# Scores from two float32r parts in quarters of the array's rows, and top-k values multiplied once a batch

## The chip, the cores and the metric

The kernel runs on one core of a Trainium2 chip. Its time is the device time of one execution in microseconds; before the change the median of three runs is 3110.93 us (3107.17 to 3118.0).

## The reference

The input is `hidden_states`, 8 batches of 1024 tokens by 128 channels, float32. Four blocks follow one another, each added to its input and each on a layer norm of it:

```
x = x + attn_a(layernorm(x))     # 16 heads of 8 channels, 1024 x 1024 softmax per head
x = x + ffn(layernorm(x))        # 128 -> 512 -> 512 -> 128, weights +1 or -1, relu
x = x + attn_b(layernorm(x))     # top-k attention, 8 heads of 16
x = x + ffn(layernorm(x))
```

In `attn_a`, q and k come from linear layers, the scores are `q k^T / sqrt(8)`, the softmax runs over all 1024 keys, and the result goes through `Wo`. In `attn_b` each token looks, for each head, at the 64 tokens up to itself. A weighted distance of queries is taken to each, the 32 nearest stay, with weights `exp(-distance)` divided by their sum, and the context is the weighted sum of the values `relu(x @ encoder_value)` of those tokens. It is multiplied by q and decoded.

## The kernel before

**Stages and turns.** Every stage of the work has a name and is written once for each engine (`go` in each engine's block), and one list of stages gives the order in which all engines issue. The lists are made by `merged` from slots with weights (`WEIGHTS`, line 119, `SPANS`, `TAIL_SPANS`); no engine departs from its list. The waits between engines are on semaphores (`Count`). A turn has two lists, one after the other. The first has the row maxima of attention for batch c (stage `max`, sides "a"), beside the last stages of attention for batch c-1 ("o"), the first FFN and the preparation of `attn_b` for c-1 ("p"), and the last FFN of c-2 ("q"). The second has the exponentials and the products with V (stages `exp`, `pvs`) of batch c, beside the top-k attention of c-1 (`SLOTS_T`: `aop`, `dist`, `dev`, `top`, `vw`, `wt`, `pv`, `st`, `dec` for each of 8 tiles of 128 tokens) and the layer norm, q, k and their splitting ("h") of batch c+1. Turns 0, 1 and 7 leave out what doesn't exist yet or any more, and a last list (`TAIL`) finishes batches 6 and 7.

**Scores.** q and k (float32) are each split into three bf16 parts (`qk` and `split`, 0 to 4): the leading part is rounded by ScalarE (ACT, line 1095), subtracted by GpSimd (POOL, 730, 733), the rest rounded again (1102) and subtracted again (737). The second half of the keys gets its sign turned as it is evicted, and the difference of the two halves, k(j) - k(j + 512), is made beside them (`kd`, 512 columns) and split in the same way. The parts are written to DRAM (`scratch_q`, `scratch_k`, lines 620 and 621) and read back into `Q` and `K`, eight rows for each part of a head, so that six products of parts are summed by one matmul: 48 rows a head (`QPART`, `KPART`, `MROW`; `load_quad`, 524). A quad is four heads; `Q[:, n, i]` holds two of them, one from row 0 and one from row 64 of the array, `par` 0 and 1, and i is 0 or 1. Rows 48 to 50 of each hold three parts of the negated maximum against rows of ones in K.

**Maxima.** A group g is 128 queries of two heads, 64 groups a batch, ordered by quad, then i, then query tile (`MAXES`, 153). PE computes for both heads the products with the key differences (512 columns, into PSUM pair 0) and the products with the far half of the keys (pair 1 or 2). ACT takes the relu of the first into `cut(g)` (line 1110), one of three slots; DVE subtracts the far products and takes the row maximum with one instruction per head (`cut_max`, 1243), for g-1 at the place of g in the list. Differences of g wait for the relu of g-1 (in turn 0, of g-2), far products of g for the maximum of g-2. Once a quad, `mrow` negates the maxima and splits them in three (five DVE instructions, 1323 to 1327), and `mturn` transposes them (876), and brings them through DRAM to the rows in Q.

**Exponentials.** A step (n, i) takes 128 keys of the quad's four heads against 512 queries: two `exp` stages, each two score matmuls of 51 rows (a PSUM pair) and one ACT exponential of 128x1024 (1123), and four products with V in column tiles of 32 (`pvs`), of which the profile shows eight records: a float32 matmul leaves two.

**Values of attn_b.** `xrev` is the layer norm's output, channels by tokens in reverse order, and its last column repeated 64 times. For each tile, `vw` multiplies four windows of 96 tokens of it with `ev` (the value encoder), and ACT evicts them with a relu into `Vw[:, n % 2]` (line 1183 calls `evict`, 1034). Neighbouring windows overlap by 64 tokens. `pv` multiplies the transposed weights `WT` with them; a column of ones beside each head's values gives the sum of the weights. `WT` lies in `Bs`, which stage `keys` uses before.

Of the kernel before, what the change touches and what calls it, by code (L numbers as in the profile page):

```python
# [22 lines left out]
P = 128  # L23
NB, T = 8, 1024
NU = T // P
HALF = 512
# [3 lines left out]
PARTS = 3  # L30
QPART = (0, 0, 0, 1, 1, 2)
KPART = (0, 1, 2, 0, 1, 0)
QLOAD = ((0, 3, 0), (3, 2, 1), (5, 1, 2))
KLOAD = ((0, 3, 0), (3, 2, 0), (5, 1, 0))
MROW = len(QPART) * HD
KT = T + HALF
# [26 lines left out]
            key=1, pad=1, an=1, qtok=1, hebb=1, dist=2, vw=1, wt=2, pv=1, st=1, dec=1)  # L63
# [46 lines left out]
def between(slots, *others):  # L110
# [5 lines left out]
    return slots  # L116


WEIGHTS = dict(O=(1.00, 0.33, 1.92, 1.58, 0.47, 1.50, 0.85, 0.85, 1.47, 2.53), P=(0.90, 0.90, 0.90, 0.90, 0.90, 0.90, 0.90, 1.08, 1.21, 1.08, 1.08, 0.63, 0.90, 0.90, 0.90, 0.39, 0.90, 0.90, 0.90, 0.90, 0.90, 0.90, 0.90, 0.90, 0.90, 1.00, 1.00, 1.00, 1.50, 0.90, 0.54, 1.08, 1.08, 1.08, 1.08, 1.08, 0.90, 0.44, 0.90, 0.90, 1.19, 1.19, 1.19, 1.19, 1.19, 1.19, 0.90, 0.90, 0.90, 1.00, 1.00, 1.00, 1.50, 0.90, 0.90, 0.90, 0.90, 0.90, 1.00, 2.00, 2.00, 1.00, 1.00, 1.00, 1.94, 2.00, 2.00, 0.48, 2.00, 2.21, 0.55, 1.10, 1.10, 1.11, 1.11), Q=(0.90, 0.90, 0.90, 0.90, 0.90, 0.90, 0.90, 1.08, 1.08, 0.75, 0.49, 1.08, 0.90, 0.90, 0.90, 0.90, 0.90, 0.90, 0.90, 0.90, 0.90, 0.90, 0.82, 0.90, 0.59, 1.00, 1.00, 1.05, 1.83, 0.05, 0.95, 1.01, 0.95, 0.90, 0.90, 0.90, 0.90, 0.90, 0.90, 0.90, 0.90, 0.90, 0.95, 0.90, 0.90, 0.90, 0.90, 0.90, 0.80, 0.90, 1.00, 1.00, 1.00, 2.18, 0.10), T=(2.57, 2.00, 2.66, 2.50, 2.00, 3.99, 1.50, 1.08, 2.57, 2.00, 2.66, 2.50, 2.00, 3.99, 1.50, 1.08, 2.57, 2.00, 2.66, 2.50, 2.00, 3.99, 1.50, 1.08, 2.17, 2.00, 2.66, 2.50, 2.00, 3.99, 1.50, 1.08, 2.57, 2.00, 2.66, 2.50, 2.00, 3.99, 1.50, 1.08, 2.57, 2.00, 2.66, 2.50, 2.00, 3.99, 1.50, 1.08, 2.57, 2.00, 2.66, 2.50, 2.00, 3.99, 2.28, 1.08, 2.57, 2.00, 2.66, 2.50, 2.00, 3.99, 1.50, 1.08, 2.57, 2.23, 2.66, 2.50, 2.00, 3.99, 1.50, 1.08, 0.86), H=(1.00, 0.75, 0.75, 0.44, 0.92, 2.48, 2.04, 1.00, 1.00, 1.00, 1.00, 0.50))
SPANS = dict(O=(0.010, 0.177), P=(0.382, 1.000), Q=(0.000, 0.453), T=(0.000, 1.000), H=(0.015, 0.300))  # L120


# [1398 lines left out]
```

## Time and profile before

| | before |
|---|---|
| runs, us | 3118.0, 3107.17, 3110.93 |
| profiled execution, us | 3113.11 |
| its span, us | 3111.4 |
| PE, DVE, ACT, POOL busy, us | 2513.3, 2152.0, 2328.1, 645.4 |
| mean granted TensorE clock | 0.907 |

Busy time is the union of an engine's instructions; the ends of matmuls are modelled, and two matmuls that run in different rows of the array overlap in it. The profile has weight loads as an engine of their own (PEld). The granted clock is a share of 2.4 GHz; 0.50 is 1.2 GHz. "Issue" among the idle times is time in which nothing that the profile shows was waited for.

### The profile page before, as it was taken

The numbers are of one execution on the slowest core, as the hardware profiler recorded it, in microseconds if no ns is written. First come the engines' busy times: TensorE is split into PE (matmuls) and PEld (weight loads), VectorE is DVE, ScalarE is ACT, GpSimd is POOL, SyncE is SP. The second block draws the span as 40 slices with busy tenths as digits, with TensorE's granted clock in tenths as the row PEclk, the third lists the DMA queues.
The fourth block names the chain that finished last, engine by engine and source line by source line (L and its number), as shares of the span: only waits on it lengthen the run. The fifth ranks groups of instructions, "written<-read, shape, count | busy, mean of one in ns | idle before, by whom it ended". The sixth has DMA issues, their size and how long they took to land.

```text
span 3111.4 us, 71098 instructions
## 1 busy us (share of the span) xinstructions
PE 2513.3 (81%) x21555; PEld 1153.9 (37%) x21555; DVE 2152.0 (69%) x10282; ACT 2328.1 (75%) x3241; POOL 645.4 (21%) x820
## 2 busy tenths in 40 slices
PE   4788788888788887888878887888878888887666
PEld 1112343344333443334433343334433344333454
DVE  5801778856786768956689467875679667982695
ACT  4798669967698677976689676995779877895433
POOL 3010114111241113301142012411124111311331
PEclk6599689999899998999999998998989999999888
DMA  2011001100011000100001000110001000000000
GB/s 87 25 45 39 2 9 40 34 18 6 9 47 34 12 13 11 51 28 9 9 33 38 18 9 9 40 34 19 12 2 60 27 8 2 9 2 1 1 8 8
DMA packets 60961, 67.50 MB, mean 22 GB/s; under 512 B 15602, under 2 KB 41908, under 8 KB 60580
## 3 DMA queue, kind: packets, MB, share of 16 engines
q1 hardware_dynamic: 60336, 62.29, 6.2%
q8 instruction: 195, 3.19, 0.4%
q14 instruction: 186, 1.52, 0.2%
q10 hardware_dynamic: 244, 0.49, 0.1%
HBM read 41.95 MB, written 20.71 MB: 20 GB/s over the span
## 4 chain that ended last, share of the span: by engine, by line
PE 38%; ACT 26%; issue 18%; DVE 11%; POOL 4%; SPq 2%; ACTq 0%; DVEq 0%; DMA 0%; POOLq 0%
PE banks L779 36%; ACT PT L1123 12%; DVE pq L1243 3%; POOL Aop L758 3%; ACT pq L1110 2%; PE banks L786 2%; ACT h L1135 2%; DVE xn L1460 1%; DVE h L1463 1%; ACT hparts L1134 1%; ACT Bs L1034 1%; ACT h L1034 1%; ACT xn L1066 1%; ACT h L1182 1%; DVE stat L1215 1%
## 5 line engine op out<-in xcount | busy, mean ns | idle before, releaser
L1123 ACT ACTIVATE PT<-banks 128x1024 f32<-128x1024 f32 x1024 | 999.9, 1035 | 85.2 <-PE banks L779 77.7
L1243 DVE CUSTOM_DVE_ANT_0 pq<-pq,banks 128x512 f32<-128x512 f32 x1024 | 656.7, 685 | 210.9 <-ACT pq L1110 164.5
L1110 ACT ACTIVATE pq<-banks 128x1024 f32<-128x1024 f32 x512 | 522.8, 1022 | 276.0 <-PE banks L779 252.6
L779 PE MATMUL banks<-PT,Vg 128*9 128x512 f32 x4096 | 550.4, 610 | 2.1 <-ACT PT L1123 2.1
L779 PE MATMUL banks<-Q,K 51*128 51x512 bf16 x2048 | 396.9, 394 | 175.8 <-ACT PT L1123 137.5
L779 PE MATMUL banks<-K,Q 48*128 48x512 bf16 x2048 | 376.3, 440 | 114.1 <-ACT pq L1110 63.9
L742 POOL TENSOR_TENSOR hparts<-h,hparts 128x512 fp32r<-128x512 f32 x112 | 140.2, 1272 | 1099.1 <-ACT h L1135 1099.0
L1460 DVE MATCH_REPLACE8 xn<-h,xn 128x96 f32<-128x96 f32 x1536 | 352.4, 243 | 0.0
L779 PE MATMUL banks<-hparts,W 128*128 128x512 f32 x1024 | 314.5, 437 | 37.1 <-ACT h L1135 30.8
L779 PEld LDWEIGHTS banks<-Q,K 51*128 51x128 bf16 x2048 | 109.5, 93 | 616.3 <-issue 584.6
L1463 DVE MAX8 h<-xn 128x8 f32<-128x96 f32 x1536 | 263.4, 244 | 0.3 <-issue 0.2
L765 POOL TENSOR_TENSOR h<-h,outside 128x768 f32<-128x768 f32 x64 | 116.7, 1823 | 643.9 <-DVE h L1443 643.9
L758 POOL TENSOR_SCALAR Aop<-qd,alpha,minus 128x128 f32<-128x128 f32 x512 | 227.1, 459 | 81.9 <-DVEq L1404 70.9
L779 PEld LDWEIGHTS banks<-hparts,W 128*128 128x128 f32 x1024 | 186.1, 200 | 138.8 <-issue 73.8
L779 PEld LDWEIGHTS banks<-K,Q 48*128 48x128 bf16 x2048 | 92.2, 96 | 371.1 <-issue 343.8
L1308 DVE TENSOR_TENSOR Vg<-banks,bvb 128x512 f32<-128x512 f32 x16 | 11.1, 692 | 180.6 <-PE banks L779 180.3
L779 PE MATMUL banks<-B,Aop 128*32 128x96 f32 x4096 | 109.6, 264 | 32.0 <-POOL Aop L758 29.4
L779 PE MATMUL banks<-xT,W 128*128 128x512 f32 x224 | 125.9, 674 | 8.7 <-ACT xT L1034 4.8
L1460 DVE MATCH_VALUE_LOAD xn<-h,xn 128x8 f32 x1536 | 123.0, 80 | 0.3
L779 PE MATMUL banks<-W,h 128*128 128x128 f32 x896 | 115.9, 282 | 6.1 <-ACT h L1034 6.1
L1134 ACT ACTIVATE hparts<-banks,scol 128x512 fp32r<-128x512 f32 x128 | 89.0, 695 | 40.7 <-PE banks L779 40.2
L1460 DVE MATCH_REPLACE8 xn<-h 128x96 f32<-128x96 f32 x512 | 117.3, 241 | 0.0
(204 smaller groups left out, 3423.7 us busy)
## 6 DMA issues: line engine op xcount, KB each, us to landing
scratch_k<-pq SPq DMA_DIRECT2D x24, 384.0 KB, 3.1
K<-scratch_k SPq DMA_DIRECT2D x126, 72.0 KB
qkf<-in_hidden_states SPq DMA_DIRECT2D x16, 512.0 KB, 4.4
scratch_q<-pq SPq DMA_DIRECT2D x24, 256.0 KB, 2.5
Q<-scratch_q SPq DMA_DIRECT2D x126, 48.0 KB
K<-scratch_k SPq DMA_DIRECT2D x126, 48.0 KB
Q<-scratch_q SPq DMA_DIRECT2D x126, 32.0 KB
out<-xr SPq DMA_DIRECT2D x14, 256.0 KB, 2.3
```

The source lines that it names most:

```text
L742: pool.tensor_tensor(h_lo[:, o, :], h1_[:, o, :], h_hi[:, o, :].bitcast(F32), ALU.subtract).then_inc((low_p if side == "p" else low_q).sem, 1)
L758: ins = pool.tensor_scalar(Aop[:, h, :], qd[:, h // 4, P * n:P * n + P], alpha[:, h:h + 1], minus1[:, h % 4:h % 4 + 1], ALU.mult, ALU.add)
L765: pool.tensor_tensor(d, d, outside[:, :].unsqueeze(1).broadcast_to([P, SH, WW]), ALU.add).then_inc(d_pool.sem, 1)
L779: return pe.matmul(o, l, r, start=start, stop=stop)
L786: ins = pe.transpose(R.bank(k)[:, P * q:P * q + P], src[:, u, :], perm)
L1034: return act.activation(dst, src, func, **kw).then_inc(R.emptied(k), 1)
L1110: act.activation(cut(g), ring_pair if work is TURN0 and g % 2 else pair[0], ACT.Relu).then_inc(diff_out.sem, 1)
L1123: act.activation(PT[:, at:at + 2, :], pair[g % ESLOTS], ACT.Exp, scale=1.0 if i % 8 < 4 else -1.0).then_inc(probs.sem, 1)
L1134: act.activation(h_hi[:, o, :], R.bank(k)[:, :], ACT.Relu, scale=scol[:, 0:1])
L1243: dve.tensor_tensor_reduce(r, r, pair[1 + g % 2][:, par, :], 1.0, -3.0e38, ALU.subtract, ALU.max, mred[:, par, i, qt:qt + 1]).then_inc(max ...
L1460: dve.match_replace(out=Rm[:, h, :], in_to_replace=m8[:, h, :], in_values=src, imm_value=-2 * BIG).then_inc(top8.sem, 1)
L1463: dve.max(out=m8[:, h, :], in_=src).then_inc(top8.sem, 1)
```

## The change

1. Scores. `PARTS` is 2 and the parts are float32r: ACT rounds to the leading part, POOL subtracts, and the rest stays in place (`qkf`, `kd`). The second rounding and subtraction are gone, `split` has two entries for five. Three products of parts are summed, 24 rows a head, and the rows of maxima are two: 26 rows. A head takes a quarter of the array's rows (`ROWS` = 32): Q and K lose their dimension i, and a quad's four heads lie at rows 0, 32, 64 and 96. The element is four bytes for two, the number of bytes loaded stays.
2. Order of groups. Groups now alternate between the two pairs of heads of a quad (`group`), so consecutive groups use other rows. PE issues the far products of g-1 right behind the differences of g (`far`), and those of the last group in a stage of their own. `mrow` and `mturn` move back by 0.8 of a group.
3. Maxima are split in two: three DVE instructions for five, one float32 transpose.
4. Values. Stage `vw` is gone. A new stage `ev`, in the slot of `hid`, multiplies each of the 8 tiles of `xrev` once, evicts them into `vrow` (which is `Bs`), POOL writes the ones, SyncE writes them to `scratch_v`, and a stage `vload` reads four windows of 96 tokens for tile n into `Vw`, one tile ahead of `wt`, `pv`.
5. `WEIGHTS` has new values in 54 of 225 slots (27 of them in T), `TAIL_SPANS` in four of five spans.
6. In the last list, the second FFN's h1 and h2 still lie in the place of Q and K, now as tensors of their own at those addresses.

```diff
-PARTS = 3
-QPART = (0, 0, 0, 1, 1, 2)
-KPART = (0, 1, 2, 0, 1, 0)
+PARTS = 2
+QPART = (1, 0, 0)
+KPART = (0, 0, 1)
 MROW = len(QPART) * HD
+ROWS = 32
...
-        (3.0, [(_u >= 2, "decd", _u - 2), (_next, "aop", _u + 1), (_last, "vw", _u - 1), (_here, "top", (_u, 0))]),
+        (3.0, [(_u >= 2, "decd", _u - 2), (_next, "aop", _u + 1), (_here, "vload", _u), (_here, "top", (_u, 0))]),
...
+def group(g):
+    return g // QGROUPS, g % 2, g // 2 % NU
+MAXES = [((g + 0.5) / GROUPS, [("a", "max", group(g))]) for g in range(GROUPS)]
+MAXES.append(((GROUPS - 0.3) / GROUPS, [("a", "far", 0)]))
+MROWS = [((min((n + 1) * QGROUPS + 0.6, GROUPS - 0.2)) / GROUPS, [("a", "mrow", n)]) for n in range(NQUAD)]
...
 def load_quad(eng, n, par, lasts):
+            for t, part, s_ in ((Q, QPART, q_s), (K, KPART, k_s)):
+                first, parts = part.index(lasts), part.count(lasts)
+                for i in range(2):
+                    r = ROWS * (2 * i + par) + HD * first
+                    eng.dma_start(t[r:r + HD * parts, n, :].bitcast(F32),
+                                  s_[lasts:lasts + 1, 4 * n + par + 2 * i].broadcast_to([parts, HD, t.shape[2]])).then_inc(quad_in[n].sem, 16)
...
+                    if stage == "ev":                                  # SyncE
+...
+                        sp.dma_start(scratch_v[0:T].rearrange("(j p) x -> p j x", p=P), ...).then_inc(v_out.sem, 16)
+                        sp.dma_start(scratch_v[T:RPAD].unsqueeze(0), ...).then_inc(v_out.sem, 16)
+                    if stage == "vload":
+                        if n == 0:
+                            sp.wait_ge(*v_out.at(b, 2))
+                        if n >= 2:
+                            sp.wait_ge(*R.filled(c, use["pv", n - 2]))
+                        for i in range(NBLK):
+                            sp.dma_start(Vw[:, n % 2, i, :, :].rearrange("p h e -> p (h e)"),
+                                         scratch_v[window(NBLK * n + i)]).then_inc(v_in[n % 2].sem, 16)
...
+                    if stage == "ev":                                  # GpSimd
+                        pool.wait_ge(*R.filled(c, k))
+                        pool.memset(vrow[:, :, :, SE:SE + 1], 1.0).then_inc(v_ones.sem, 1)
...
+            def products(dst, g, keys):                                # TensorE
+                n, i, qt = group(g)
+                for par in range(2):
+                    r = ROWS * (2 * i + par)
+                    ins = mm(dst[:, par, :], Q[r:r + MROW, n, P * qt:P * qt + P], K[r:r + MROW, n, keys])
+                return ins
+            def far(b, g):
+                if g == 1:
+                    pe.wait_ge(*o_out.at(b, 0))
+                if g >= 2:
+                    pe.wait_ge(*max_out.at(b, g - 1))
+                products(pair[1 + g % 2], g, slice(HALF, T)).then_inc(far_in.sem, 1)
...
+                        differences = products(diff, g, slice(T, KT))
+                        differences.then_inc(diff_in.sem, 1)
+                        if g >= 1:
+                            far(b, g - 1)
...
                     if stage == "exp":
...
-                            rows_ = slice(64 * par, 64 * par + MROW + PARTS)
-                            ins = mm(pair[g % ESLOTS][:, par, :], K[rows_, n, j, P * (i % 8):P * (i % 8) + P],
-                                     Q[rows_, n, j, HALF * (i // 8):HALF * (i // 8) + HALF])
+                            r = ROWS * (2 * j + par)
+                            rows_ = slice(r, r + MROW + PARTS)
+                            ins = mm(pair[g % ESLOTS][:, par, :], K[rows_, n, P * (i % 8):P * (i % 8) + P],
+                                     Q[rows_, n, HALF * (i // 8):HALF * (i // 8) + HALF])
...
-                    if stage == "vw":
-                        one(c, k, [(R.bank(k)[0:WW, P * i:P * i + P], xrev[:, window(NBLK * n + i)], ev[:, :], True, True)
-                                      for i in range(NBLK)])
+                    if stage == "ev":
+                        for i in range(2):
+                            one(c, k + i, [(R.bank(k + i)[:, P * q:P * q + P], xrev[:, P * (4 * i + q):P * (4 * i + q) + P], ev[:, :], True, True)
+                                           for q in range(4)])
...
                     if stage == "keys":                                # DVE, before the first write to Bs
+                        dve.wait_ge(*v_out.at(b, 2))
```

## Rows read from the trace of the kernel before

**Rows 1.** The page's first part: busy us, share of the span, instructions.

```profile
PE 2513.3 (81%) x21555; PEld 1153.9 (37%) x21555; DVE 2152.0 (69%) x10282; ACT 2328.1 (75%) x3241; POOL 645.4 (21%) x820
```

**Rows 2.** Stretches: length, busy us (instructions) of each engine, granted clock, DMA share, GB/s.

```profile
55.00:150.00 95.00, 69.71 (x268) 12.22 (x270) 85.37 (x291) 67.50 (x70) 0.00 (x0) 0.50 0.11 37
150.00:290.00 140.00, 115.51 (x777) 24.61 (x774) 0.84 (x5) 132.57 (x154) 14.41 (x8) 0.96 0.12 41
...
1188.00:1375.00 187.00, 154.77 (x1911) 60.45 (x1911) 147.69 (x883) 168.05 (x216) 53.95 (x72) 0.97 0.10 33
1375.00:1563.00 188.00, 151.22 (x806) 82.06 (x809) 128.46 (x427) 124.94 (x193) 30.60 (x34) 0.93 0.04 11
2660.00:3111.00 451.00, 337.40 (x3598) 187.94 (x3597) 308.33 (x1833) 268.33 (x407) 110.86 (x153) 0.89 0.02 5
```

**Rows 3.** Groups by line and form, 1188:1375: busy us, mean ns | idle before.

```profile
L1123 ACT ACTIVATE PT<-banks 128x1024 f32<-128x1024 f32 x128 | 125.4, 1036 | 9.9 <-PE banks L779 9.4
L1034 ACT ACTIVATE Vw<-banks 96x512 f32<-96x512 f32 x8 | 4.8, 598 | 1.1 <-PE banks L779 1.0
...
L779 PE MATMUL banks<-Q,K 51*128 51x512 bf16 x256 | 49.2, 391 | 22.5 <-ACT PT L1123 18.1 <-DVE mred L1243 3.9 <-issue 0.2
L779 PE MATMUL banks<-ev,xrev 128*96 128x128 f32 x64 | 8.8, 281 | 0.0
```

**Rows 4.** Waits of 1188:1375 (two) and of 1375:1563: us in total, times, longest.

```profile
ACT PT L1123 <- PE banks L779: 9.4, 12, 3.7
...
PE banks L779 <- ACT PT L1123: 18.3, 36, 1.5
...
ACT pq L1110 <- PE banks L779: 34.8, 29, 6.8
```

**Rows 5.** Groups by line and form, 1375:1563: score matmuls, weight loads.

```profile
L779 PE MATMUL banks<-K,Q 48*128 48x512 bf16 x256 | 42.6, 399 | 11.9 <-ACT pq L1110 7.5 <-DVE mred L1243 3.5 <-issue 0.2
...
L779 PEld LDWEIGHTS banks<-hparts,W 128*128 128x128 f32 x128 | 22.9, 199 | 17.5 <-issue 12.2 <-ACT h L1034 1.8 <-POOL hparts L742 0.4
L779 PEld LDWEIGHTS banks<-K,Q 48*128 48x128 bf16 x256 | 11.4, 94 | 40.4 <-issue 36.8
```

**Rows 6.** PE in order of time: start us, us, line, operation, count.

```profile
1414.30 1.20 PE L779 MATMUL banks<-hparts,W 128*128 128x512 f32 x4
...
1419.95 0.60 PE L779 MATMUL banks<-K,Q 48*128 48x512 bf16 x4
1420.48 1.72 PE L779 MATMUL banks<-W,h 128*128 128x128 f32 x13
...
1505.21 2.05 PE L779 MATMUL banks<-W,h 128*128 128x128 f32 x16 [0.24 <-ACT h L1034]
```

**Rows 7.** The same view: a lone transpose in float32, one in bf16.

```profile
1401.16 0.30 PE L918 MATMUL banks<-ident,on 128*128 128x128 f32 x1 [0.43 <-ACT h L1034]
...
1475.92 0.22 PE L876 MATMUL banks<-identb,mb 128*96 128x128 bf16 x1
```

**Rows 8.** The same view in an exponential stretch: PV products, weight loads, score matmuls.

```profile
1300.73 1.05 PE L779 MATMUL banks<-PT,Vg 128*9 128x512 f32 x8
...
1301.71 0.10 PEld L779 LDWEIGHTS banks<-Q,K 51*128 51x128 bf16 x2 [0.86 <-issue]
...
1346.49 0.92 PE L779 MATMUL banks<-Q,K 51*128 51x512 bf16 x4
```

**Rows 9.** Groups by line and form, whole span: second rounding and subtraction, maxima split.

```profile
L737 POOL TENSOR_TENSOR pq<-qkf,pq 128x1024 bf16<-128x1024 f32 x16 | 34.8, 2178 | 15.6 <-ACT pq L1102 15.1
...
L1102 ACT ACTIVATE pq<-qkf 128x1024 bf16<-128x1024 f32 x16 | 16.8, 1052 | 2.5 <-POOL qkf L730 2.5
...
L1325 DVE TENSOR_TENSOR nm<-nm,mb 128x32 f32<-128x32 f32 x32 | 13.4, 419 | 1.1
```

**Rows 10.** POOL and SyncE at the start, in order of time.

```profile
29.60 4.82 POOL L737 TENSOR_TENSOR pq<-qkf,pq 128x1024 bf16<-128x1024 f32 x2
...
36.60 0.32 SPq L620 DMA_DIRECT2D scratch_q<-pq  x1
```

More of the change, by code:

```diff
@@ L187, in phases @@
     order = merged(*one) + merged(*two)
-    assert not ahead or order.index(("h", "split", 4)) < order.index(("h", "load", 0))
+    assert not ahead or order.index(("h", "split", 1)) < order.index(("h", "load", 0))
     if twice:
@@ L455, in hybrid_block_kernel @@
         gn_l = count("gate_ln", 1)
+        v_ones = count("value_ones", 1)
+        v_out = count("values_out", 2, 16)
+        v_in = [count(f"values_in{i}", NU // 2, 16 * NBLK) for i in range(2)]
         e_steps = count("e_steps", 2 * NU)
@@ L464, in hybrid_block_kernel @@
         xb_a = count("bias_added", 1)
-        act_a = count("part_rounded", 6)
-        pool_a = count("part_left", 6)
+        act_a = count("part_rounded", 3)
+        pool_a = count("part_left", 3)
         kd_a = count("keys_subtracted", 1)
-        split_out = [count(f"split_out{part}", 2, 16) for part in range(PARTS)]
-        quad_in = [count(f"quad{n}_in", 1, 24 * 16) for n in range(NQUAD)]
+        split_out = [count(f"split_out{part}", 3, 16) for part in range(PARTS)]
+        quad_in = [count(f"quad{n}_in", 1, 16 * 16) for n in range(NQUAD)]
         m_red = count("max_split", NQUAD)
@@ L862, in go @@
                                 pass_waits(pe)
-                        for dst, keys in ((diff, slice(T, KT)), (pair[1 + g % 2], slice(HALF, T))):
-                            if dst is not diff and g >= 2:
-                                pe.wait_ge(*max_out.at(b, g - 1))
-                                pass_waits(pe)
-                            for par in range(2):
-                                rows_ = slice(64 * par, 64 * par + MROW)
-                                ins = mm(dst[:, par, :], Q[rows_, n, i, P * qt:P * qt + P], K[rows_, n, i, keys])
-                            ins.then_inc((diff_in if dst is diff else far_in).sem, 1)
+                        differences = products(diff, g, slice(T, KT))
+                        differences.then_inc(diff_in.sem, 1)
+                        if g >= 1:
+                            far(b, g - 1)
+                    if stage == "far":
+                        far(b, GROUPS - 1)
                     if stage == "mturn":
```

183 lines of the change are left out of this document (91 added, 92 removed).

## The prediction

> **What bounds the kernel now.** I read the clock and busy shares of the page first, then the span by stretches, then the groups of two stretches, their waits, and single instructions in order of time. TensorE (PE) is busy for 81% of the span of 3111.4 us [rows 1]; the profiled execution took 3113.1 us. That average hides two kinds of stretch, which the split by stretches shows [rows 2]: for each batch a stretch of row maxima (188 us where the rows show one, 1375:1563) and a stretch of exponentials (187 us, 1188:1375). There are seven such pairs in which the back stages of an earlier batch run beside the scores; the first batch's pair (55:150 and 150:290) is nearly bare, and after about 2840 only back stages are left.
>
> In the exponential stretch ScalarE (ACT) is busy 168 of 187 us and PE 155: ACT sets the pace. Of its 19 idle us, 9.4 are waits of the exponential for PE, and PE waits 18.3 us for the exponential [rows 4]: the two pass the pace to each other through two PSUM pairs. In the maxima stretch PE is busy 151 of 188 us against 125 for ACT and 128 for VectorE (DVE) [rows 2], and ACT's largest wait is 34.8 us for PE [rows 4]. PE sets it. In the first maxima stretch DVE is busy 85 of 95 us and the clock is at 0.50, the 1.2 GHz level; that one is DVE's.
>
> **The change, part by part.**
>
> *Values once a batch (stage vw to ev).* Gone from each exponential stretch: 64 records of ev products, 8.8 us of PE, and 8 evictions of 598 ns, 4.8 us of ACT [rows 3]. Added to the maxima stretch: 8 products, 16 records of 128 columns, at the pitch of such records (2.05 us for 16, 0.128 each [rows 6]) 2.1 us of PE, and two evictions, 1.2 us of ACT, which its 34.8 us wait for PE covers. The memset on POOL stands between work it waits for anyway (30.6 busy of 188 us [rows 2]). The DMAs (34 per batch, 0.6 MB out and 1.7 MB back) meet a DMA share of 0.04 to 0.10 [rows 2]. SyncE gets them in exchange for 32 fewer K and Q issues (64 for 96) and 8 more for the maxima; a window is asked for more than one tile, over 20 us, before pv. Cost nothing; if that cover failed, pv and behind it PE would wait a DMA round trip for each of eight tiles, a few us a turn. The DVE stage "keys" now waits for the values to leave Bs; in the queue behind it stand the max reductions, but ten slots of P lie between.
>
> *Two parts for three.* The three second roundings go from ACT: two whole and one half tile at 1052 ns a whole, 2.6 us, in the exponential stretch; POOL loses 2.5 times 2178 ns, 5.4 us [rows 9], work that can stand ahead of the Aop operands. I count POOL's at nothing (bounds: 0 and -2 us a turn). Two of five small DVE steps per quad go, 8 times 0.42 us a turn [rows 9]; DVE bounds neither stretch, so nothing (bounds 0 and -3.4). K and Q bytes stay the same: half the rows, twice the width.
>
> *The price of float32r weights.* A bf16 weight load of these scores takes 94 ns, a float32r one (hparts) 199 ns [rows 5]. What of it a matmul feels: a lone transpose of 128 columns took 0.22 us in bf16 and 0.30 us in float32 [rows 7], so +0.08 us where the load isn't covered. In the exponential stretch it isn't: the score's load begins 0.98 us after the start of the PV products that take 1.05, not during them [rows 8]. 128 pairs at +0.08 are +10.2 us of PE. From below it is 0 (covered), from above the whole difference twice over, if the two loads of a pair queue: 2 x 0.199 - 0.094 = +0.30 a pair. No row shows float32r in row tiles; I take 0.08, from the nearest row with a lone load.
>
> The Trainium skill (TensorE: Matmul & The Clock Gate, "Weight-path perf modes") says that the fast weight load needs 128 weights and a type that isn't FP32, and so speaks against this change: it would put the float32r load at its full column time. [...]
>
> *Heads in quarters, far of g-1 behind differences of g.* Today four score matmuls come as two pairs after one another: 0.60 us, and the next group starts 0.53 us after the first [rows 6]. The two matmuls of a pair run together and take as long as one, 0.39 us (mean of one 0.391 [rows 3]), so the second pair costs 0.21, 512 columns at 2.4 GHz. After the change the four stand in four different row quarters and can stream together: 0.53 - 0.21 + 0.08 = 0.40 us a group. 64 groups: -8.3 us of PE a maxima stretch. Bounds: -13.4 (loads covered), and if they ran like the float32r stream of hparts, (1.20 - 0.39)/3 = 0.27 each [rows 6], 0.39 + 3 x 0.27 = 1.20 against 0.60, +38.
>
> **The sum**, against 3113.1:
> - Exponential stretch, seven times. ACT -4.8 - 2.6 = -7.4; PE -8.8 + 10.2 = +1.4. ACT paces, PE takes its 1.4 back: -6 each.
> - Maxima stretch, seven times. PE -8.3 + 2.1 = -6.2; PE is busy 80% of it, the rest waits that need not shrink: -5 each.
> - First batch: maxima 0 (DVE); exponentials only the roundings, -2.6 (ACT busy 132.6 of 140 [rows 2]).
> - Start: the last part was written at 36.60, after POOL's second subtractions that began at 29.60 [rows 10]; now there are none: -7.
> - End: 8.8 us of PE go from a stretch where neither PE nor DVE is full; half of it, -4.
>
> -77 - 2.6 - 7 - 4 = -91, which gives 3022. The median shown is 2 us under the profiled execution: 3020. With the bounds above per turn (-2 to -20), this case runs from 2970 to 3080.
>
> **The rivals.**
>
> *A: loads hidden, quarters truly parallel.* Consecutive pairs use other quarters in both stretches, so loads could enter beside running matmuls, and two exponential pairs issued late (0.92 us for four today, where the second pair had waited a little [rows 8]) could overlap. Then PE -8.8 in the exponentials (phase -9) and -13.4 + 2.1 in the maxima (phase -10): 7 x 19 + 14 = 147, 2964. For it: the two 94 ns loads of a pair end together today. Against: nothing was loaded during PV [rows 8].
> The Trainium skill (TensorE: Matmul & The Clock Gate, "The mechanism" of packing) has it that weight loads overlap running matmuls only when the row group differs. By that rule this case would be the right one; no row here shows quarters, so it gets its own chance only.
>
> *B: the new order takes it back.* DVE's maximum of g-1 could start when ACT's relu of g-1 ended. Now it needs far(g-1), which PE issues behind diff(g), which waits for that same relu: at least 0.39 us later, and later still when PE is behind. On DVE the layer norm factors and the attention's division stand behind it, on which PE and ACT wait. If 0.17 of the 0.39 us reach the pace of a group, 64 x 0.17 = 11 us a turn cancel all: 3111 give or take 9.
>
> *C, slower: float32r row tiles load one after another.* Place: every score group. Price: exponentials +0.30 x 128 - 8.8 = +30 of PE, some +20 after idle time; maxima, four loads 0.80 for the 0.09 of today's first pair, less the 0.21 of the second stream: +0.50 x 64 = +32, plus 2, some +27. Seven times 47: about 3430. It decides from where a pair costs +0.15 and a group is over 0.60 us. For it: the load row, doubled; against it, PV's column tiles in float32, eight records, are through in 1.05 us [rows 8], so tiles as such can load and run beside one another.
>
> *D, slower: the clock.* The first maxima stretch ran at 0.50 with PE busy 70 of 95 us, the later ones at 0.93 with 151 of 188 [rows 2]. Less streaming per group might let it fall more often. At a mean of 0.80 PE's work in such a stretch grows by 0.93/0.80, 16% or 24 us; 8 of it go into idle time, 16 stay, against the 11 won: +5 a turn less the 14 of start and end, and in the exponential stretches some loss too: 3140.
>
> **Chances.** Forecast 0.53, A 0.22, B 0.10, C 0.08, D 0.07. A difference of 0.3% (9 us) is what a measurement of this kernel can tell. Forecast, A and a little of B and D are faster: 0.77. Same: 0.09, mostly B. Slower: 0.14, C, most of D, the rest of B. The range leaves out C, the worse half of D and the far end of A: 2940 to 3115.
>
> **What would show it.** Right: maxima stretches some 5 us shorter, with four score matmuls in about 0.40 to 0.50 us; a float32r score load of about 0.2 us; exponential stretches near 181, ACT still over 85% busy; the first maxima some 7 us earlier. Wrong: a group of four over 0.6 us (C), DVE's maximum waiting long for PE (B), a lower clock in the maxima stretches (D), or stretches 9 and 10 us shorter (A).

## The result: slower by 2.1%

| | before | after |
|---|---|---|
| median, us | 3112.65 (4 runs, 3107.17 to 3118.0) | 3176.57 (4 runs, 3170.8 to 3184.19) |
| ratio to before | | 1.0207, interval 1.0178 to 1.0236 |
| span of the profiled execution, us | 3111.4 | 3176.9 |
| mean granted TensorE clock | 0.907 | 0.872 |

Every median and profile in this document is of executions in the chip's usual state; one execution of bf16_rows32, 3621.18 us at a mean clock of 0.546, was in a slow one and is left out.

The page after, first part and row of the clock. It answers to [rows 1]: ScalarE, VectorE and GpSimd are busy for less time, TensorE for 115.5 us more.

```profile
PE 2628.8 (83%) x21171; PEld 1306.8 (41%) x21171; DVE 2081.0 (66%) x10218; ACT 2288.2 (72%) x3169; POOL 603.2 (19%) x802
...
PEclk6588688989789898989889888899978989999887
```

Stretches of the kernel after, with the columns of [rows 2]. I now cut them at events, so that both kernels can be added up: a stretch of maxima (M) begins with the first relu of a batch, one of exponentials (E) with its first exponential; the last E ends where the last exponential starts. In order: first M, first E, an E, an M, an E, an M.

```profile
52.80:140.90 88.10, 77.79 (x261) 34.05 (x257) 80.96 (x271) 65.66 (x68) 0.00 (x0) 0.50 0.12 40
140.90:295.70 154.80, 136.04 (x802) 38.04 (x801) 3.92 (x23) 134.99 (x156) 9.57 (x5) 0.90 0.12 42
...
847.80:1037.30 189.50, 167.67 (x1850) 66.78 (x1849) 139.05 (x872) 161.29 (x204) 45.21 (x66) 0.90 0.14 45
1037.30:1223.80 186.50, 153.84 (x797) 93.39 (x797) 120.67 (x406) 123.16 (x193) 28.88 (x31) 0.91 0.06 15
1223.80:1408.60 184.80, 164.47 (x1855) 66.21 (x1854) 139.40 (x872) 161.48 (x204) 45.07 (x65) 0.92 0.15 45
1408.60:1595.80 187.20, 151.47 (x794) 91.43 (x792) 120.31 (x405) 123.15 (x192) 28.89 (x31) 0.91 0.06 15
```

The stretch of the kernel before that answers to the third line, cut in the same way:

```profile
826.00:1011.00 185.00, 156.75 (x1915) 60.59 (x1913) 145.01 (x873) 167.59 (x216) 51.05 (x69) 0.95 0.11 34
```

In E, PE was busy 157 and ACT 168 of 185 us; now it is PE 168 and ACT 161 of 189.5, so PE is now the busier of the two. Added up over the seven later batches (us; one profile each, so that a few us of a difference can be chance: scale_only below has the instructions of the kernel before, and its sums differ by 3 and 5 us):

| | start | first M | first E | M, seven | E, seven | tail |
|---|---|---|---|---|---|---|
| before | 52.9 | 92.5 | 145.9 | 1261.8 | 1265.5 | 292.8 |
| after | 52.8 | 88.1 | 154.8 | 1295.9 | 1292.3 | 293.0 |
| forecast | -7 | 0 | -2.6 | -35 | -42 | -4 |
| measured | 0 | -4.4 | +8.9 | +34 | +27 | 0 |

The groups of the whole span after, by line and form (busy us, mean ns | idle time before, and what ended it):

```profile
L1174 ACT ACTIVATE PT<-banks 128x1024 f32<-128x1024 f32 x1024 | 1000.4, 1034 | 156.9 <-PE banks L818 154.5
L1295 DVE CUSTOM_DVE_ANT_0 pq<-pq,banks 128x512 f32<-128x512 f32 x1024 | 656.9, 685 | 391.2 <-PE banks L818 363.2 <-ACT pq L1161 14.4 <-issue 10.3
...
L818 PE MATMUL banks<-Q,K 26*128 26x512 f32 x2048 | 497.2, 521 | 149.3 <-ACT PT L1174 116.4 <-DVE mred L1295 26.4 <-issue 1.0
L818 PE MATMUL banks<-K,Q 24*128 24x512 f32 x2048 | 369.3, 557 | 86.0 <-ACT pq L1161 62.0 <-DMA K<-scratch_k 11.3 <-ACT mT L1089 6.8
...
L818 PEld LDWEIGHTS banks<-Q,K 26*128 26x128 f32 x2048 | 204.6, 192 | 639.3 <-issue 618.9
```

The first four of these before:

```profile
L1123 ACT ACTIVATE PT<-banks 128x1024 f32<-128x1024 f32 x1024 | 999.9, 1035 | 85.2 <-PE banks L779 77.7
L1243 DVE CUSTOM_DVE_ANT_0 pq<-pq,banks 128x512 f32<-128x512 f32 x1024 | 656.7, 685 | 210.9 <-ACT pq L1110 164.5 <-issue 20.1 <-PE banks L779 17.1
...
L779 PE MATMUL banks<-Q,K 51*128 51x512 bf16 x2048 | 396.9, 394 | 175.8 <-ACT PT L1123 137.5 <-DVE mred L1243 29.1 <-issue 2.5
L779 PE MATMUL banks<-K,Q 48*128 48x512 bf16 x2048 | 376.3, 440 | 114.1 <-ACT pq L1110 63.9 <-DVE mred L1243 34.1 <-DMA K<-scratch_k 8.0
```

The exponential itself takes the same 1034 ns; its waits for PE doubled, 77.7 to 154.5 us. The maximum's waits for PE went from 17.1 to 363.2 us, which looks like the cause and, as the experiments show, is not. The scores of the exponentials take 100 us more of PE; those of the maxima, which were to take 66 less, take 7 less.

### The profile page after: what moved, and what is told of

Its sections match the earlier page's. It is cut to its first block, busy times and chain, and to the rows that moved or that the text cites. A ratio compares the mean times of both kernels' runs of the same rounds, so it can differ in the third digit from the quotient of the medians.

```text
span 3176.9 us, 70321 instructions
## 1 busy us (share of the span) xinstructions
PE 2628.8 (83%) x21171; PEld 1306.8 (41%) x21171; DVE 2081.0 (66%) x10218; ACT 2288.2 (72%) x3169; POOL 603.2 (19%) x802
## 4 chain that ended last, share of the span: by engine, by line
PE 43%; ACT 25%; issue 16%; DVE 9%; POOL 3%; SPq 1%; DMA 1%; ACTq 0%; DVEq 0%; POOLq 0%
PE banks L818 40%; ACT PT L1174 12%; ACT pq L1161 3%; DVE pq L1295 3%; POOL Aop L797 2%; PE banks L825 2%; ACT xn L1121 1%; ACT Bs L1089 1%; SPq L545 1%; DVE xn L1511 1%; ACT h L1089 1%; ACT hparts L1185 1%; DVE h L1514 1%; ACT pq L1121 1%; ACT oT L1179 1%
## 5 line engine op out<-in xcount | busy, mean ns | idle before, releaser
L1174 ACT ACTIVATE PT<-banks 128x1024 f32<-128x1024 f32 x1024 | 1000.4, 1034 | 156.9 <-PE banks L818 154.5
L1295 DVE CUSTOM_DVE_ANT_0 pq<-pq,banks 128x512 f32<-128x512 f32 x1024 | 656.9, 685 | 391.2 <-PE banks L818 363.2
L818 PE MATMUL banks<-Q,K 26*128 26x512 f32 x2048 | 497.2, 521 | 149.3 <-ACT PT L1174 116.4
L818 PE MATMUL banks<-PT,Vg 128*9 128x512 f32 x4096 | 580.6, 641 | 1.6 <-ACT PT L1174 1.6
L818 PEld LDWEIGHTS banks<-Q,K 26*128 26x128 f32 x2048 | 204.6, 192 | 639.3 <-issue 618.9
L818 PE MATMUL banks<-K,Q 24*128 24x512 f32 x2048 | 369.3, 557 | 86.0 <-ACT pq L1161 62.0
L818 PEld LDWEIGHTS banks<-K,Q 24*128 24x128 f32 x2048 | 169.1, 210 | 316.3 <-issue 289.4
L818 PE MATMUL banks<-B,Aop 128*32 128x96 f32 x4096 | 128.5, 292 | 35.3 <-POOL Aop L797 24.0
L818 PE MATMUL banks<-xT,W 128*128 128x512 f32 x224 | 134.0, 715 | 23.0 <-DVE xr L1419 13.9
L818 PEld LDWEIGHTS banks<-B,Aop 128*32 128x32 f32 x4096 | 110.7, 132 | 57.5 <-POOL Aop L797 31.0
```

Source lines behind the costliest of these rows:

```text
L818: return pe.matmul(o, l, r, start=start, stop=stop)
L1174: act.activation(PT[:, at:at + 2, :], pair[g % ESLOTS], ACT.Exp, scale=1.0 if i % 8 < 4 else -1.0).then_inc(probs.sem, 1)
L1295: dve.tensor_tensor_reduce(r, r, pair[1 + g % 2][:, par, :], 1.0, -3.0e38, ALU.subtract, ALU.max, mred[:, par, i, qt:qt + 1]).then_inc(max ...
```

## The experiments

Every run was timed beside the kernel before on the same chip. "Rows" below are rows of the array that a score matmul reads. The stretch table at the end of this section has the sums of all that matter.

**values_only**: the kernel before with only part 4, values once a batch, and the slot weights of before. The edit in words:

```diff
-stage vw: products of xrev windows with ev for each tile, evicted into Vw
+stage ev: 8 products a batch into vrow, scratch_v; stage vload: four windows from scratch_v into Vw
```

> The kernel before with the values made once a batch (stages ev and vload for vw), scores in three bf16 parts, old slot weights. If the loss lies in the scores, this alone gains what the prediction's terms of the values give: per turn ACT -4.8 and PE -8.8 in the exponential stretch, +2 PE in the maxima, so about -4 a turn, 3075 to 3090. If instead the values' DMAs, their waits or the Bs tile's new use cost the time, it is at 3113 or above, up to 3176.

Measured: 3103.82 us, 0.9969 (0.9953 to 0.9984). E lost 37 us, 5.3 a turn, about ACT's 4.8 that the prediction gave it. M gained 24 us, 3.4 a turn, where the prediction had hidden the evictions' 1.2 and PE's 2.1 was the only cost. The expected 3075 to 3090 was missed for it. Two more pairs of runs differ in the values alone, and the price in M isn't the same in them: from before_rows64 to values_rows64 M gains 13.6 and E loses 38.8, from scores_only to after M gains 4.6 and E loses 50.1.

**scores_only**: the kernel after with stage vw of before in place of part 4. The edit in words:

```diff
-stages ev, vload, scratch_v
+stage vw, as before
```

> The changed kernel with the values as they were before (vw for ev and vload), new scores, new order, new weights. If the loss lies in the scores: 3176 plus what the values gain, 3195 to 3215. If it lies in the values: 3113 or less.

Measured: 3224.02 us, 1.0347 (1.0301 to 1.0392). The loss is in the scores, and 77 of its 111 us are in E. Beside these scores the values save 47 us (3224.02 to 3176.57), in the kernel before they saved 9: work taken off PE and ACT in E is worth more now. That vw's products count for more because PE has less room is argued, not tried.

**far_together**: far(g) right behind the differences of g, aimed at rival B.

```diff
-                        if g >= 1:
-                            far(b, g - 1)
...
-                    if stage == "far":
-                        far(b, GROUPS - 1)
+                        far(b, g)
```

> The changed kernel with the far products of g issued right behind the differences of g, as before; groups still alternate between the pairs of heads, and differences and far products of one group then use the same two quarters. If the late far products (DVE waits 363 us for PE instead of 17) made the maxima stretches longer: those go back by about 5 us each, 3140. If weight loads and the clock are the cause: no gain, and PE pays 0.2 us more for each of 64 groups, up to 3200.

Measured: 3280.94 us, 1.0553 (1.0513 to 1.0593), clock 0.847. Its groups of maxima scores and of the maximum:

```profile
L1292 DVE CUSTOM_DVE_ANT_0 pq<-pq,banks 128x512 f32<-128x512 f32 x1024 | 656.5, 685 | 265.2 <-ACT pq L1158 232.8 <-issue 16.5 <-PE banks L818 8.0
...
L818 PE MATMUL banks<-K,Q 24*128 24x512 f32 x2048 | 442.9, 539 | 107.4 <-ACT pq L1158 45.9 <-DVE mred L1292 44.5 <-DMA K<-scratch_k 11.7
```

DVE's waits for PE fell from 363.2 to 8.0 us, and the kernel was 104 us slower. The run doesn't settle rival B by itself, as it changes a second thing: the second pair now reads the rows that the first one is using, and PE's scores take 74 us more. The late far products are a gain on the whole, with float32r weights. What speaks against B without this flaw is the next run.

**bf16_read**: the kernel after, its score matmuls reading the upper halves of the same float32r words as bf16. Rows, bytes, order, stages and slot weights stay; lower bits of the scores are left out.

```diff
+            def hi(t, rows_, n, lo, up):
+                return t[rows_, n, lo:up].bitcast(BF16).rearrange("p (c two) -> p c two", two=2)[:, :, 1]
...
-                    ... Q[r:r + MROW, n, P * qt:P * qt + P], K[r:r + MROW, n, keys])
+                    ... hi(Q, slice(r, r + MROW), n, P * qt, P * qt + P), hi(K, slice(r, r + MROW), n, keys.start, keys.stop))
```

> The changed kernel with the score matmuls reading only the upper 16 bits of each float32r element of Q and K, as bf16 with a stride of two; same tiles, rows, order, DMAs. It leaves out the lower bits of the scores. If the exposed float32r weight load (a pair 0.49 instead of 0.39 us) is the cause: a pair returns to 0.39, exponential stretches lose some 8 us each, total 3080 to 3110. If the lower clock comes from fewer rows in use and is the cause: the clock stays near 0.87 and the time at 3150 to 3180.

Measured: 3101.23 us, 0.9958 (0.9944 to 0.9972), 75 us below the kernel after: 43 of it in E, 19 in M, 7 in the first E. Its maximum and its two groups of the exponentials' scores:

```profile
L1298 DVE CUSTOM_DVE_ANT_0 pq<-pq,banks 128x512 f32<-128x512 f32 x1024 | 656.9, 685 | 366.0 <-PE banks L818 336.5 <-ACT pq L1164 13.8 <-issue 10.8
...
L818 PE MATMUL banks<-Q,K 26*128 26x512 bf16 x2048 | 404.7, 411 | 187.6 <-ACT PT L1177 154.0 <-DVE mred L1298 24.6 <-issue 1.0
...
L818 PEld LDWEIGHTS banks<-Q,K 26*128 26x128 bf16 x2048 | 108.9, 92 | 686.7 <-issue 665.4
```

192 ns a load became 92, and the scores' busy time fell from 497.2 to 404.7 us: 92.5 us over 1024 pairs is 0.09 a pair. The maxima's scores, not shown as a line, fell from 369.3 to 305.5 us, 0.12 for each of 512 groups. The float32r operands are the greatest single cause, and of them the load: far_together, whose pairs of a group stand on the same rows, takes 0.73 us for four at full clock, where the kernel before takes 0.60 for such a group in bf16. The second pair costs 0.23 us against 0.21, so the streaming is nearly the same, and the 0.11 us by which a single pair is longer is about the 0.10 by which its load is longer. Such a group of far_together:

```profile
1502.78 0.73 PE L818 MATMUL banks<-K,Q 24*128 24x512 f32 x4
```

Two rivals fall here. DVE still waits 336.5 us for PE in the new order, and M is 9 us shorter than in values_only; B's 11 us a turn would have to be hidden by a gain of 86 us in M, which no run shows. And the mean clock stayed at 0.877, near the 0.872 of the kernel after, with 75 us less: the lower mean clock by itself doesn't make the loss.

**old_weights**: the kernel after with `WEIGHTS` and `TAIL_SPANS` of the kernel before.

> The changed kernel with WEIGHTS and TAIL_SPANS as before. If the new order of the slots cost time (the first 50 us of each exponential stretch are the slow ones): faster than 3176, 3150. If it was worth something: slower, 3185 to 3210. The theories of weight load and clock say nothing of it.

Measured: 3264.28 us, 1.0502 (1.0482 to 1.0522). The new weights are worth 88 us to this kernel; they hide no loss.

**waits_first**: both waits of far(g-1) ahead of the differences of g.

```diff
-            def far(b, g):
+            def far_waits(b, g):
...
+                        if g >= 1:
+                            far_waits(b, g - 1)
                         differences = products(diff, g, slice(T, KT))
```

> The changed kernel with the wait for the far products of g-1 passed before the differences of g, so that PE issues four score matmuls with no wait between them. If the 0.25 us between the two pairs (a group took 0.74 us where PE had been waiting, 0.51 where it had work behind it) is the issue of that wait: groups go to 0.51, about half of 64 groups win 0.23, 7 us a turn of PE and 20 to 40 us in all, 3140 to 3155. If the second pair is held by its weight loads instead: no change, 3176.

Measured: 3185.2 us, 1.0232 (1.0215 to 1.0249). First the kernel after, PE in a maxima stretch in order of time (start us, us), its loads beside it:

```profile
1458.13 0.51 PE L818 MATMUL banks<-K,Q 24*128 24x512 f32 x4
...
1458.13 0.19 PEld L818 LDWEIGHTS banks<-K,Q 24*128 24x128 f32 x4
...
1459.80 0.46 PEld L818 LDWEIGHTS banks<-K,Q 24*128 24x128 f32 x4 [0.94 <-issue]
...
1459.83 0.74 PE L818 MATMUL banks<-K,Q 24*128 24x512 f32 x4
```

Of the 62 groups issued as four in the M at 1408.6, 26 take about 0.51 us and 27 take 0.72 or more; in the second case the second pair's loads come 0.25 us late, with the far wait between the pairs. With the waits first, nearly every group at full clock takes about 0.51:

```profile
L818 PE MATMUL banks<-K,Q 24*128 24x512 f32 x2048 | 303.0, 571 | 162.9 <-ACT pq L1167 94.7 <-DVE mred L1301 31.2 <-issue 15.8
```

PE's scores fell by 66 us, its waits for the relu rose from 62.0 to 94.7, and M got no shorter (1307.9 against 1295.9). Taking time off PE's scores doesn't shorten M. (Adding 74 us to them in far_together went with 76 us more of M, at a lower clock, 0.847 in the mean.)

**bf16_waits_first**: both edits together.

> Both: score matmuls that read the upper 16 bits as bf16 (the lower bits of the scores left out), and the far wait passed before the differences. If load and wait are separate costs they add up: 3101 minus 20 to 40, 3060 to 3080. If one hides the other: 3095 to 3101.

Measured: 3116.49 us, 1.0005 (0.9994 to 1.0016), 15 us above bf16_read. Without the float32r load, too, the earlier waits bring nothing.

**few_rows**: the kernel before, reading 24 and 26 rows of each half for 48 and 51; the exponential's scale keeps numbers small. Same instructions, same columns, same loads.

```diff
-                                rows_ = slice(64 * par, 64 * par + MROW)
+                                rows_ = slice(64 * par, 64 * par + 24)
...
-                            rows_ = slice(64 * par, 64 * par + MROW + PARTS)
+                            rows_ = slice(64 * par, 64 * par + 26)
...
-                                       scale=1.0 if i % 8 < 4 else -1.0).then_inc(probs.sem, 1)
+                                       scale=0.1 if i % 8 < 4 else -0.1).then_inc(probs.sem, 1)
```

> The kernel before (bf16, pairs at rows 0 and 64) with only the first 24 of 48 rows of a head multiplied in the maxima and 26 of 51 in the exponentials; it leaves out the lower parts of the scores and the maximum, and the exponential's scale is 0.1 so that it stays finite. Same instructions, columns and order. If the clock goes by how many rows of the array work: it falls from 0.907 towards 0.88 and the time rises by 15 to 40 us, 3130 to 3150. If not: 3113, clock 0.907, and the fall in the changed kernel comes from its idle time on PE.

Measured: 3301.03 us, 1.0604 (1.0541 to 1.0667), clock 0.828 for 0.907. A kernel whose matmuls read fewer rows is 187 us slower, far beyond the 15 to 40 us expected. An exponential stretch of it, to be held against that of before at 826.00, with the same number of matmuls:

```profile
871.10:1074.50 203.40, 176.77 (x1916) 67.13 (x1913) 143.29 (x873) 167.94 (x216) 50.98 (x69) 0.84 0.10 31
```

**scale_only**: the scale alone.

> The kernel before with the exponential's scale at 0.1 and all rows; the attention weights are then not the reference's. Control for few_rows. If rows were the cause there: 3113 and clock 0.907. If the data (exponentials near 1 rather than near 0) were: 3200 or more and a clock near 0.83.

Measured: 3110.91 us, 0.9994 (0.9982 to 1.0005), clock 0.912. The scale isn't the cause.

**few_rows_max**: 24 rows in the differences and far products alone.

> The kernel before with only 24 of 48 rows of a head multiplied in the maxima (it leaves out products of the lower parts in the maxima, the exponentials are whole and unscaled). If the number of rows at work sets the clock: it falls in the maxima stretches (0.93 before) and each gets some us longer, 3140 to 3180, exponential stretches unchanged. If few_rows was slow for its scaled exponentials: 3113.

Measured: 3212.13 us (3177.86 to 3223.94), 1.0334 (1.0298 to 1.0371); the profiled execution was the fastest of four. An E and the M behind it:

```profile
1212.30:1396.10 183.80, 155.30 (x1915) 60.07 (x1913) 144.51 (x873) 167.52 (x215) 51.06 (x69) 0.96 0.11 34
1396.10:1594.60 198.50, 171.06 (x783) 89.31 (x779) 123.16 (x412) 122.90 (x191) 28.62 (x30) 0.80 0.03 10
```

Only the stretches whose rows were cut got a lower clock, and got longer (M +66 in sum, E -2). The exponentials' data are untouched here.

**rows32**: the kernel after, its exponential scores reading all 32 rows of a quarter, where rows 26 to 31 are zeros written once at the start; they add nothing to a sum.

```diff
-                            rows_ = slice(r, r + MROW + PARTS)
+                            rows_ = slice(r, r + ROWS)
...
+            dve.memset(Q[:, :, :].bitcast(F32), 0.0)
+            dve.memset(K[:, :, :].bitcast(F32), 0.0).then_inc(zeroed, 1)
```

> The changed kernel with the exponential's score matmuls over all 32 rows of a quarter; rows 26 to 31 of Q and K are zeroed once at the start. If the rows that a matmul uses keep the clock up whatever is in them: clock above 0.872, exponential stretches 2 to 5 us shorter, 3140 to 3165. If a row of zeros counts for nothing, or rows are not the cause: 3176 to 3185 (the zeroing at the start costs a few us).

Measured: 3138.5 us, 1.009 (1.0072 to 1.0108), 38 us below the kernel after though the zeroing costs 6.6 at the start; clock 0.897 for 0.872. By the two profiles E is 28 and M 17 us shorter. The E that answers to 847.80 after, and the M behind it, which answers to 1037.30:

```profile
838.80:1023.70 184.90, 162.51 (x1851) 66.26 (x1849) 138.95 (x871) 161.25 (x205) 45.36 (x65) 0.93 0.15 46
1023.70:1207.10 183.40, 148.97 (x797) 89.95 (x797) 120.70 (x406) 123.27 (x192) 28.75 (x30) 0.94 0.05 15
```

189.5 us at 0.90 became 184.9 at 0.93, and the M behind it went from 186.5 us at 0.91 to 183.4 at 0.94, though its own matmuls read no more rows. The clock is lowest in the first 50 us of an E, shown here for the kernels before and after and for rows32:

```profile
826.00:876.00 50.00, 40.43 (x406) 15.01 (x404) 42.60 (x244) 44.40 (x62) 18.81 (x25) 0.86 0.04 16
```

```profile
847.80:897.80 50.00, 43.08 (x382) 17.66 (x380) 36.30 (x232) 41.71 (x57) 14.52 (x19) 0.77 0.05 11
```

```profile
838.80:888.80 50.00, 42.66 (x393) 16.79 (x390) 38.63 (x251) 44.14 (x60) 16.15 (x21) 0.83 0.05 11
```

**bf16_rows32**: rows32 and bf16_read together.

> The same 32 rows with the matmuls reading the upper 16 bits as bf16 (lower bits of the scores left out). Same question at the bf16 weight load: 3075 to 3095 if rows keep the clock up, 3101 to 3110 if not.

Measured: median 3101.26 us (3089.5 to 3109.95), 0.9964 (0.9941 to 0.9987), clock 0.884, no better than bf16_read by the median. Its first relu comes 6.9 us later than in bf16_read, for the zeroing, so the rows may give back that much. The two gains don't add: 38 us beside float32r loads, zeroing paid, and none clear of the scatter beside these bf16 loads. Its profiled execution was short (span 3088.5) and that of bf16_read long (3108.3), so the stretches flatter it.

**before_rows64**: the kernel before, with zeros written once, reading 64 rows in the exponentials and the differences.

```diff
-                                rows_ = slice(64 * par, 64 * par + MROW)
+                                rows_ = slice(64 * par, 64 * par + (64 if dst is diff else MROW))
...
-                            rows_ = slice(64 * par, 64 * par + MROW + PARTS)
+                            rows_ = slice(64 * par, 64 * par + 64)
```

> The kernel before, with the exponential's matmuls and the differences in the maxima over all 64 rows of a half of the array (the rows beyond 51 and 48 are zeros in K, zeroed once at the start, so nothing is left out). If rows keep the clock up in bf16 too: clock above 0.907 and 10 to 25 us less, 3090 to 3103, in spite of some 3 us for the zeroing. If above 48 rows more don't count: 3113 to 3117.

Measured: 3108.97 us, 0.9981 (0.9971 to 0.9991), clock 0.919: a gain, but less than the 10 to 25 us expected. The first relu comes 5.4 us later for the zeroing.

**values_rows64**: values_only and before_rows64 together.

> The same with the values made once a batch. If both gains stand beside each other: 3080 to 3092, faster than before, the change and every experiment so far. If rows don't count above 48: 3104 to 3108.

Measured: 3081.64 us (3075.09 to 3083.95), 0.9891 (0.9873 to 0.9909), clock 0.914. It beats both kernels: 1.1% below the kernel before, 3% below the kernel after. Against values_only the 64 rows are worth 22 us, zeroing paid, where against the kernel before they were worth 5.

| sums, us | M, seven | E, seven | clock | median |
|---|---|---|---|---|
| before | 1261.8 | 1265.5 | 0.907 | 3112.65 |
| values_only | 1285.7 | 1228.4 | 0.897 | 3103.82 |
| scores_only | 1291.3 | 1342.4 | 0.869 | 3224.02 |
| after | 1295.9 | 1292.3 | 0.872 | 3176.57 |
| bf16_read | 1276.6 | 1249.7 | 0.877 | 3101.23 |
| waits_first | 1307.9 | 1288.7 | 0.871 | 3185.2 |
| far_together | 1371.9 | 1303.3 | 0.847 | 3280.94 |
| rows32 | 1278.9 | 1264.7 | 0.897 | 3138.5 |
| few_rows | 1357.7 | 1361.0 | 0.828 | 3301.03 |
| few_rows_max | 1327.7 | 1263.6 | 0.878 | 3212.13 |
| scale_only | 1258.9 | 1260.7 | 0.912 | 3110.91 |
| bf16_rows32 | 1262.8 | 1242.3 | 0.884 | 3101.26 |
| before_rows64 | 1260.2 | 1254.0 | 0.919 | 3108.97 |
| values_rows64 | 1273.8 | 1215.2 | 0.914 | 3081.64 |

## Why the prediction was wrong

The forecast was -91 us and faster, 3020 with a range of 2940 to 3115; 3176.57 was measured, and the profiled spans differ by +65.5. The 156 us between them: 69 in the exponential stretches, 69 in the maxima, 7 in the first batch, 11 in start and end.

**The step that failed first: "ACT paces, PE takes its 1.4 back: -6 each".** The size of the load was nearly right. The pair was to cost +0.08 us, and bf16_read shows 0.09; single pairs took 0.50 us in the later stretches where they had taken 0.39. The rule of the Trainium skill (TensorE: Matmul & The Clock Gate, "Weight-path perf modes"), that the fast load isn't for FP32 types, agrees: 192 ns against 92 in two kernels that differ only in how the score matmuls read their operands. What was wrong was to take PE's 10.2 us a turn as lying beside ACT's pace, so that next to nothing of it would show (PE's net 1.4 a turn); 6.1 a turn showed (42.6 over seven E). PE and ACT don't pass through an E side by side: PE waits for an exponential, computes a pair, ACT waits for that pair. PE in an E after, in order of time:

```profile
1303.62 0.50 PE L818 MATMUL banks<-Q,K 26*128 26x512 f32 x2
...
1304.36 0.21 PEld L818 LDWEIGHTS banks<-Q,K 26*128 26x128 f32 x2 [0.56 <-issue]
...
1304.39 0.50 PE L818 MATMUL banks<-Q,K 26*128 26x512 f32 x2 [0.27 <-ACT PT L1174]
1304.82 1.05 PE L818 MATMUL banks<-PT,Vg 128*9 128x512 f32 x8
```

The load begins only when the exponential has released the pair, so it lies in the loop between the two engines and not beside it. In the first E, which has next to nothing else in it, 128 pairs at 0.09 to 0.10 would be 12 to 13 us: +8.9 was measured, against the -2.6 forecast, a difference of 11.5. bf16_read takes 7.3 of it back, so some of the load is hidden even there. The rows that I had read allowed this: ACT's 9.4 us of waits and PE's 18.3 [rows 4] said that both stood in the loop, and I wrote that sentence, then gave the whole turn to ACT. From run to run, one profile each, E goes from 1265.5 by -37.1 (values), +21.3 (two parts, quarters, new order and new slot weights, read as bf16) and +42.6 (float32r reads) to 1292.3. The first and the last step are single edits; the middle one is all the rest of the change at once. Against the forecast's -33.6, -18.2 and +9.8 that is 3.5 better, 39.5 worse and 32.8 worse: 69 in sum. So the load that was charged too low is half of it. The other half is the step "two parts for three, ACT -2.6", where ACT's roundings did go and E got longer; what made it longer isn't separated.

**The clock, rival D, had a cause, at the wrong place and price.** It bears on that other half. I tied it to PE's busy share in the maxima, gave it 3140 and 0.07. What matters as well is how many rows a matmul reads, and the exponentials went from twice 51 to twice 26. That the number of rows, with the instructions alike, changes clock and time, is shown by few_rows, few_rows_max and scale_only; that it acts in the kernel after, by rows32: 28 us of E, 17 of M. These 28 and the 43 of the load overlap: beside bf16 loads in quarters the rows gave no clear gain, so the 39.5 us are not shown to be the rows' at all. Nor is it a rule that bf16 loads leave nothing to gain: from values_only to values_rows64 the rows gave 22 us. A slow clock lengthens each pair, and should be felt most where PE has the least room, which the float32r load brought about; that link is argued, not shown by a run of its own. The Trainium skill (TensorE: Matmul & The Clock Gate, "Part 1: The HAM clock gate") lets the gate follow how busy PE has been. The E of few_rows, PE busy 177 of 203 us at 0.84 against 157 of 185 at 0.95, shows that busy time alone doesn't decide.

**"Maxima -5 each: PE sets it" failed.** With single profiles: before 1261.8, +23.9 for the values, +19.3 for the float32r loads (after less bf16_read), which leaves -9.1 for the quarters, the shorter split of the maxima, the new order and the new slot weights together. As the price of the values in M ranges from 4.6 to 23.9 between pairs of runs, that remainder is rough too. The term "quarters, -8.3 a turn" was 13.4 for the quarters less 5.1 for the loads. Both parts missed: on PE the quarters with bf16 reads saved 8.9 a turn (376.3 to 305.5 us), and float32r took 0.12 us a group back, 8.0 a turn, so 0.9 a turn was left. What the quarters lack is the time between the pairs of nearly half of the groups, 0.25 us, which the step had not counted: without it, in waits_first, PE's scores fell to 303.0 us even in float32r. But there M was no shorter; nor did 71 us less of them in bf16_read bring M more than 9 below values_only. So the reading behind it was wrong as well: 34.8 us of ACT's waits for PE [rows 4] don't say that less score work moves M. That PE works through the back stages ahead of those scores would explain it, but wasn't tried. ACT's waits in the M at 1408.6 after are 30.5 us, a like number with another kernel.

**Values once a batch** was right in E (5.3 a turn for 4.8) and wrong in M (3.4 a turn for nothing net of the quarters' gain; PE 2.1 and ACT 1.2, "which its 34.8 us wait for PE covers"). So idle time of ACT may be no cover for evictions that stand in its queue between relus; that is argued. The sum, 3.3, fits the 3.4, but by luck in part: the same edit costs M 1.9 a turn between before_rows64 and values_rows64 and 0.7 between scores_only and after. The DMAs and the memset showed no wait of size, as forecast.

**Start.** The last part left earlier, as forecast, but its loads hardly did. SyncE's queue after, and the time from issue to landing of the transfer in between:

```profile
31.31 0.32 SPq L632 DMA_DIRECT2D scratch_q<-qkf  x1
...
41.69 0.64 SPq L545 DMA_DIRECT2D Q<-scratch_q  x2
```

```profile
scratch_k<-xT SPq DMA_DIRECT2D x1, 256.0 KB, 9.5
```

The write that had been issued at 36.60 [rows 10] goes out at 31.31. The part now has 1280 KB to write (512 of q, 768 of k and the key differences) where the third bf16 part had 640, and the differences' 256 KB, issued last, land after 9.5 us; the last write before took 6.0. The loads of this part start at 41.69, against 43.16 before, and the first relu comes at 52.8 for 52.9; PE waits 11.3 us for K, where it waited 8.0. So POOL's 5 us went into this transfer and the loads behind it. Why the transfer takes so long stays open. **End**: -4 forecast, 0.2 longer measured; neither engine full there was no ground for half of the 8.8 us.

With -2 and -20 us a turn and the other terms as they stand, the forecast's case runs from 2957 to 3083, not from 2970 to 3080; nothing hangs on it.

**The rivals.** A (loads hidden) and C (loads of row tiles one after another) are both false: four loads of a group took 0.19 us together, and a pair 0.50, between A's 0.39 and C's 0.69 (0.39 + 0.30). B is false by bf16_read, with the new order and M shorter than in values_only. Of the marks that the prediction named, the load of about 0.2 us and the group near 0.50 (nearly half of them) came true, and so did ACT over 85% busy in the exponentials (161.29 of 189.50 us), which didn't show what it was to show. The exponentials near 181, shorter maxima stretches and the earlier start failed. The lower clock in the maxima (D) came true in part, 0.91 and 0.91 for 0.93, and "the maximum waiting long for PE (B)" came true without its meaning: both were bad marks.

**Still open**: why the values cost M 24 us beside old scores and 5 beside new ones; why rows32 raised the clock of M, too, which reads no more rows there; which part of the change (rows, quarters, order, slot weights) made E 21 us longer with bf16 reads and less work for ACT; why more rows help so little in bf16_rows32 and by 22 us in values_rows64; whether what counts is the rows of one matmul or of all that stand side by side (M after has four times 24, M before twice 48, and its clock is 0.91 at 1037.30).

## What to carry to other kernels

- When two engines wait for each other in turn through a small set of buffers, the busier one isn't "the" bound: of a cost between release and refill a good part is paid every round (here 6.1 of some 11.5 us a turn), whatever idle time the engine shows. Look at where in the loop the new piece begins, not at the engine's total.
- Before packing matmuls into fewer rows, read the granted clock by stretch; if fewer rows lower it, reading zeroed rows up to the tile's edge may cost one memset and give it back (38 us, 22, 5 and nothing clear in the four kernels tried here).
- A long wait is not a cost until a kernel without it is faster; here the longest new one was part of a gain.

## What the hardware showed that I had not expected

- The granted clock depends on the rows that matmuls read, at equal counts and columns: 0.907 with 48 and 51 rows twice, 0.828 with 24 and 26, 0.919 with 64 in two of three kinds of scores. Rows of zeros count. In time: +187 us, and -5. All these runs have pairs of matmuls at rows 0 and 64.
- Four float32r row tiles load in 0.19 us, no longer than one of 192 ns, when nothing stands between them; with a wait between the pairs the four take 0.46. With bf16 reads, too, such a wait makes 0.64 of 0.40 us for the matmuls.
- A bf16 read of every second element keeps the short load: 92 ns, as against 94 packed [rows 5]. The Trainium skill (TensorE: Matmul & The Clock Gate, "Weight-path perf modes") allows steps up to 1,024 elements, which agrees.
- A float32r pair on 26 rows takes 0.50 us at full clock against 0.39 in bf16; the difference is about that of the loads, 0.10. A second pair behind it on the same rows costs 0.23 us, in bf16 0.21.
- At the clock of 0.50 a pair of score matmuls is 0.79 us for 0.50, and the eight PV records 1.90 for 1.05, in an E after:

```profile
1242.52 0.79 PE L818 MATMUL banks<-Q,K 26*128 26x512 f32 x2
...
1246.09 1.90 PE L818 MATMUL banks<-PT,Vg 128*9 128x512 f32 x8
```
